# A gated cross-attention layer with a quantised feed-forward: first loads reordered, first query tiles in chunks, last batch's layers behind its last projection

## The chip, the cores and the metric

One core of a Trainium2 chip runs the whole program. Its engines are TensorE (PE; its weight loads are listed as PEld), VectorE (DVE), ScalarE (ACT), GpSimd (POOL) and SyncE (SP, which issues nearly all of the DMAs). The metric is the device time of one execution in microseconds.

## What is computed

For each of 16 batches of 512 tokens with 512 features, and 120 context rows of 384 features:

```python
q = layernorm(x) @ Wq + bq ; k = ctx @ Wk + bk ; v = ctx @ Wv + bv      # 16 heads of 32
x1 = x + tanh(g_xattn) * (softmax(q k' / sqrt(32)) v @ Wo + bo)
h = layernorm(x1) ; s = max(amax(|h|), 1e-6) / 127 ; z = round(h / s)  # per token
out = x1 + tanh(g_ffn) * ((z @ Wq8') * s * w_scale + bias)
```

## The kernel before

Every engine runs one list of instructions that is written out by hand; engines wait for each other by semaphores. A batch has 4 query tiles (or chunks) of 128 rows. `on`, `probs`, `xt`, `x_in`, `cen` and the two `x1` tiles are in SBUF, and there are 8 PSUM banks: `scores` (4), `pv_ps`, `sum_ps`, `bank_a`, `bank_b`. Products of float32 are made of three passes of a high and a low part (`three`, L315); the high part is a copy by ACT (`high_x`, `high_wq`), the low part a subtraction by DVE (`low_x`, L1008) or POOL (`wq_lo`, L1461).

The **front** (batch 0 and the preparation of batch 1) goes so. SP issues the loads in the order Wq, four tiles of `x` of batch 0, context, Wk, the transposed `x` (`xt`), and more behind it; ACT issues six small ones first, among them the gates and the biases. TensorE runs 22 float32 products of 128x128 that nobody reads (`keep_running`, L320), then the column means of Wq (L630). DVE makes the layernorm statistics of the four tiles (`x_statistics`, L981), then subtracts the means from Wq in four chunks (`centre_wq`, L994); POOL makes the reciprocal deviations, which TensorE spreads over the partitions (`spread_rstd`, L430). Keys of a pair of batches follow (`project_k`, L337), and as soon as `xt` has landed, DVE scales its chunks (`scale_x0`, L990), ACT and DVE split them, and `project_q(0, 0)` uses a chunk as it comes. `scores_by_query` (L354) gives the row maxima to DVE (`maxima`, L1018, on one set of score banks, so the next tile's scores wait for them). The maxima of all four tiles are split (`high_max`, `low_max`), turned by TensorE (`turn_max`, L362) and copied (`copy_max`), and `step(0)` starts with `scores_by_key` (L369, L373).

`step(i)`, for batches 0 to 14, holds the attention of batch i, the output projection and the quantised layer of batches i-1 and i-2, and the queries of batch i+1. In it POOL makes `q_xs` in two small operations per half batch (`quant_units`, L1334 and L1336). In step 0 `fold_bias` (L437) multiplies the value bias by Wo, for DVE (`fold_rows`) and for the residual loads of SP.

The **end** (`last_step`, `turns_and_layers`) has batch 15's attention and projection, and the quantised layers of batches 14 (m) and 15 (LAST). For each tile t of LAST: `residual` (L1036), statistics, `centre_last` (ACT, L753), `quant_max_last` (DVE), `quant_factors_last` (DVE), `round_last` (ACT, L758), `integers_last` (ACT, L763), `turn_last` (PE, L410), `copy_zt_last` (ACT, L767), `last_layer` (PE, L416), `dequantise_own` (DVE, L1083), and at the end `add_out_last` (DVE, L1089; tiles 1 to 3) or `add_own` (POOL, L1358; batch 14, and tile 0), and the store. Batch 14's second half is turned by `turn_z` (L404), copied by `copy_zt` (L773) and multiplied by `quantised_layer` (L422).

## Time and profile before

| | us |
|---|---|
| time, median of 3 runs | 850.18 |
| lowest and highest of them | 847.35, 850.35 |
| time of the profiled execution | 847.59 |
| its span, first to last instruction | 845.8 |
| TensorE busy in the span | 824.4 (97%) |
| DVE, ACT, POOL busy | 536.3, 512.1, 517.5 |
| mean granted TensorE clock | 0.998 of full |

The profiled execution is one execution, 2.6 us below the median; 1.8 us of its time lie outside the span. TensorE's busy share counts overlapped, modelled durations, so that it says little of single waits; those are read in the timeline.

### The profile page before, as it was taken

To read this page: it belongs to the slowest core of one execution; us is meant where nothing else is said; L and a number is where in the kernel's file an instruction comes from. 1 tells how busy PE (TensorE), PEld (TensorE's weight loads), DVE (VectorE), ACT (ScalarE), POOL (GpSimd) and SP (SyncE) were. 2 spreads that over 40 slices of the span, in tenths; PEclk is the share of its full clock that TensorE was granted. 3 is DMA by queue.
4 is the path that set the end of the run, shared out by engine and by line. 5 is a ranking of instruction groups with operands and counts; after the bars stand their busy time and mean duration, and the time that the engine had idled before them with its cause. 6 is when DMAs were issued, how large, how long until landed. Compare 5 with 4: busy or idle time off the path is not lost.

```text
span 845.8 us, 16173 instructions
## 1 busy us (share of the span) xinstructions
PE 824.4 (97%) x6356; PEld 518.8 (61%) x6356; DVE 536.3 (63%) x754; ACT 512.1 (61%) x711; POOL 517.5 (61%) x560
## 2 busy tenths in 40 slices
PE   8999999999999999999999999999999999999995
PEld 6755566656656656666666666656666666655553
DVE  5764658566567666558566566766657655555567
ACT  4465566665665656566566665666566565666674
POOL 3526475574767647495674768557485674655687
PEclk9999999999999999999999999999999999999999
DMA  8522604223241421314232241422315131111112
GB/s 323 165 54 97 193 26 137 76 87 107 68 132 52 153 77 38 126 51 155 76 97 83 76 138 50 138 76 60 121 51 162 38 89 50 38 51 50 51 51 100
DMA packets 39179, 79.62 MB, mean 94 GB/s; under 512 B 6848, under 2 KB 7488, under 8 KB 37056
## 3 DMA queue, kind: packets, MB, share of 16 engines
q1 hardware_dynamic: 37808, 77.74, 28.6%
q8 instruction: 50, 0.82, 0.4%
q10 hardware_dynamic: 1296, 0.86, 0.3%
q14 instruction: 25, 0.20, 0.1%
HBM read 61.78 MB, written 16.81 MB: 93 GB/s over the span
## 4 chain that ended last, share of the span: by engine, by line
PE 70%; DVE 15%; POOL 4%; issue 4%; ACT 3%; DMA 2%; SPq 1%; DVEq 0%; POOLq 0%; ACTq 0%
PE bank_b L315 22%; PE bank_a L315 12%; PE scores L354 8%; PE pv_ps L383 7%; PE sum_ps L385 6%; PE scores L369 5%; DVE row_max L1018 5%; DVE xt_lo L1008 4%; PE bank_a L422 3%; DVE u_sb L1096 2%; PE bank_a L337 2%; POOL x L1340 2%; DMA xt<-in_x_t 1%; PE scores L373 1%; PE bank_b L337 1%
## 5 line engine op out<-in xcount | busy, mean ns | idle before, releaser
L1018 DVE TENSOR_REDUCE row_max<-scores 128x16 f32<-128x1920 f32 x64 | 138.1, 2158 | 122.7 <-PE scores L354 122.7
L1353 POOL TENSOR_TENSOR x<-x,u_sb 128x512 f32<-128x512 f32 x56 | 75.6, 1350 | 159.4 <-DVE u_sb L1096 157.2
L715 ACT ACTIVATE probs<-scores 120x2048 f32<-120x2048 f32 x64 | 120.4, 1881 | 65.2 <-PE scores L373 64.9
L1344 POOL TENSOR_TENSOR o_lo<-on,o_hi 128x512 fp32r<-128x512 f32 x63 | 86.7, 1378 | 68.9 <-ACT o_hi L731 68.4
L1008 DVE TENSOR_TENSOR xt_lo<-xt,xt_hi 128x512 fp32r<-128x512 f32 x64 | 66.5, 1059 | 65.5 <-ACT xt_hi L678 65.3
L1348 POOL TENSOR_TENSOR x<-x,gbias_r 128x512 f32<-128x512 f32 x64 | 82.0, 1280 | 36.6 <-ACT cen L737 35.6
L1297 POOL TENSOR_TENSOR xt<-xt,rstd_b 128x512 f32<-128x512 f32 x60 | 92.6, 1571 | 3.4 <-ACT rstd_b L952 2.1
L354 PEld LDWEIGHTS scores<-k_sb,q_sb 32*128 32x128 f32 x2048 | 62.9, 186 | 51.7 <-issue 51.2
L1340 POOL TENSOR_TENSOR x<-x,gbo_r 128x512 f32<-128x512 f32 x64 | 89.5, 1409 | 1.2 <-DMA x<-in_x 1.0
L731 ACT ACTIVATE o_hi<-on 128x512 fp32r<-128x512 f32 x64 | 40.4, 632 | 73.2 <-DVE on L1031 73.0
L369 PE MATMUL scores<-q_sb,k_sb 32*120 32x512 f32 x512 | 72.6, 636 | 5.2 <-DVE row_max L1018 3.0
L354 PE MATMUL scores<-k_sb,q_sb 32*128 32x120 f32 x2048 | 74.7, 282 | 0.1
L721 ACT ACTIVATE inv_sum<-sum_ps 128x512 f32<-128x512 f32 x64 | 38.2, 597 | 56.7 <-PE sum_ps L385 56.7
L383 PE MATMUL pv_ps<-probs,v_sb 120*32 120x512 f32 x512 | 68.2, 605 | 1.9 <-ACT probs L715 0.3
L1047 DVE TENSOR_REDUCE q_amax<-cen 128x1 f32<-128x513 f32 x60 | 38.8, 683 | 44.3 <-POOL cen L1311 42.9
L385 PE MATMUL sum_ps<-probs,ones_f 120*32 120x512 f32 x512 | 66.6, 592 | 0.0
L742 ACT ACTIVATE cen<-cen,magic,q_rec 128x512 f32<-128x512 f32 x60 | 45.5, 806 | 31.3 <-DVE q_rec L1056 31.3
L315 PE MATMUL bank_a<-xt_hi,wq_hi 128*128 128x512 f32 x128 | 54.1, 423 | 1.2 <-DVE xt_lo L1008 1.0
L315 PE MATMUL bank_b<-xt_hi,wq_hi 128*128 128x512 f32 x128 | 53.8, 420 | 0.3
L315 PE MATMUL bank_b<-wo_hi,o_hi 128*128 128x512 f32 x124 | 53.1, 429 | 0.0
L373 PE MATMUL scores<-max_t,pick 8*120 8x512 f32 x256 | 51.9, 790 | 0.0
L315 PE MATMUL bank_b<-xt_hi,wq_lo 128*128 128x512 f32 x128 | 50.6, 395 | 0.0
(185 smaller groups left out, 1801.5 us busy)
## 6 DMA issues: line engine op xcount, KB each, us to landing
xt<-in_x_t SPq DMA_DIRECT2D x16, 1024.0 KB, 5.5
x<-in_x SPq DMA_DIRECT2D x64, 256.0 KB, 2.9
out_x<-x SPq DMA_DIRECT2D x61, 256.0 KB, 2.1
x_in<-in_x SPq DMA_DIRECT2D x60, 256.0 KB, 4.1
rstd_b<-rstd_rows SPq DMA_DIRECT2D x14, 256.0 KB, 4.9
ctx_sb<-in_ctx_t SPq DMA_DIRECT2D x8, 360.0 KB, 5.2
probs<-in_wq SPq DMA_DIRECT2D x1, 1024.0 KB, 5.7
x<-in_wo SPq DMA_DIRECT2D x1, 1024.0 KB, 11.7
```

The source lines that it names most:

```text
L315: ins = pe.matmul(out_ap, stat[a], mov[b], start=first and p == 0, stop=last and p == PASSES - 1)
L354: ins = pe.matmul(scores[:, r, t * KEYS:(t + 1) * KEYS], q_sb[STRIPS[r], j, t * P:(t + 1) * P], k_sb[n // 2 % 2][STRIPS[r], j, keys_of(n)] ...
L369: pe.matmul(scores[0:KEYS, r], k_sb[i // 2 % 2][STRIPS[r], j, keys_of(i)], q_sb[STRIPS[r], j], start=True, stop=False)
L383: pe.matmul(pv_ps[STRIPS[r], :], v_sb[i % 3][0:KEYS, h], probs[0:KEYS, r], start=True, stop=True)
L385: ins = pe.matmul(sum_ps[STRIPS[r], :], ones_f[0:KEYS, :], probs[0:KEYS, r], start=True, stop=True)
L715: act.activation(probs[0:KEYS], scores[0:KEYS], ACT.Exp, scale=SCALE).then_inc(p_ready, 1)
L1008: dve.tensor_tensor(xt_lo[:, c], xt[:, c], xt_hi[:, c].bitcast(F32), ALU.subtract).then_inc(x_split, 1)
L1018: dve.tensor_reduce(row_max[:].rearrange("p (t r) j -> p r t j", r=ROWG)[:, :, :, j], scores[:, :, 0:QT * KEYS].rearrange("p r (t k) -> p ...
L1297: pool.tensor_tensor(by_tile, by_tile, rstd_b[:].rearrange("q (p t) -> q t p", t=QT), ALU.mult).then_inc(x_scaled, 1)
L1340: pool.tensor_tensor(x1_of(n)[:, t], x1_of(n)[:, t], gbo_r[:], ALU.add).then_inc(xb_ready, 1)
L1344: pool.tensor_tensor(o_lo[i % 2][:, j], on[:, j % 2], o_hi[i % 2][:, j].bitcast(F32), ALU.subtract).then_inc(o_split, 1)
L1348: pool.tensor_tensor(x1_of(m)[:, t], x1_of(m)[:, t], gbias_r[:], ALU.add).then_inc(x1b_ready, 1)
```

## The change

- **Loads.** SP issues Wq, then the context, the left half of Wk (columns 0 to 255), the four tiles of `x`, the right half of Wk, `xt`. The biases, `picks` and the gates are no longer issued by ACT ahead of everything, but by SP behind `xt`. ACT's tanh of the gates moves from the start to behind the second query bias, with a table load on each side.
- **TensorE, front.** 14 unread products instead of 22. Keys of tiles 0 and 1 come before `spread_rstd(0)`. Query tiles 0 and 1 take turns chunk by chunk. The last chunk of the values of batch 1 moves behind `turn_max(0)`, the last chunk of `fold_bias` behind `turn_max(1)`.
- **DVE and ACT, front.** `low_x(1, 0)` moves behind `low_max(0)`; `high_max(0)` and `copy_max(0)` move ahead of `high_x(1, 2)` and `high_x(1, 3)`.
- **q_xs.** The division by 127 moves into the row `gws_r`, and one of POOL's two operations per half batch goes.
- **End.** The projection of LAST's tiles 2 and 3 comes before batch 14's quantised layers, with `turn_z` of batch 14's second half between the two. That half has a tile of its own (`zt_own`, in the free `k_sb`). LAST's quantisation takes its lower bound in `quant_factors_last` (three small DVE operations instead of two), so that `cen_last` needs no 513th column, and POOL loses four of its six small operations per tile. The eight dequantisations stand behind all of LAST's factors on DVE, and POOL's `add_own` behind all of its `bias_x1`.

```diff
@@ -230,11 +231,17 @@
     load(wq_landed, wq_stage[:], rows(wq))
+    load_ctx(0)
+    load(wk_landed[0], wk_sb[:, :, 0:D // 2], rows(wk)[:, :, 0:D // 2])
     for t in range(QT):
         load(x0_landed[t], x0_stage[t], x_v[0, t])
-    load_ctx(0)
-    load(wk_landed, wk_sb[:], rows(wk))
+    load(wk_landed[1], wk_sb[:, :, D // 2:D], rows(wk)[:, :, D // 2:D])
     load_xt(0)
+    load(bk_landed, bk_c[:], bk)
+    load(bq_landed, bq_c[:], bq)
+    load(picks_landed, picks[:], consts_pick)
+    load(gates_landed, gates[:, 0:1], g_xattn.partition_broadcast(P))
+    load(gates_landed, gates[:, 1:2], g_ffn.partition_broadcast(P))
     for t in range(QT):
@@ -416,6 +423,13 @@
+    def quantised_layer_own(m, t, bank):
+        pe.wait_ge(zt_ready, nth(m, 2, t // 2))
+        for c in range(DT):
+            at = ((t % 2) * DT + c) * P
+            ins = pe.matmul(bank[:], zt_own[:, at:at + P], w8_b[:, c], start=c == 0, stop=c == DT - 1)
+        ins.then_inc(ffn_done, 1)
@@ -430,13 +444,14 @@
-    def fold_bias(bank):
+    def fold_bias(bank, chunks):
         pe.wait_ge(wo_gated, 1)
         pe.wait_ge(bv_landed, 16)
-        for c in range(DT):
+        for c in chunks:
             ins = pe.matmul(bank[:], bv_c[:, c:c + 1].broadcast_to([P, P]), wo_stage[:, c],
                             start=c == 0, stop=c == DT - 1)
-        ins.then_inc(bv_ready, 1)
+            if c == DT - 1:
+                ins.then_inc(bv_ready, 1)
@@ -551,10 +566,12 @@
         if i == 0:
-            fold_bias(bank_b)
+            fold_bias(bank_b, range(DT - 1))
         if is_batch(b):
...
             turn_max(b, pv_ps)
+        if i == 0:
+            fold_bias(bank_b, range(DT - 1, DT))
         if is_batch(m):
@@ -594,51 +611,53 @@
             add_heads(i, t, DT - 1, scores[:, t]).then_inc(proj_done, 1)
+        project_o(i, 2, scores[:, 2])
+        pe.wait_ge(log_done, nth(i, DT, 3))
+        turn_z(m, 1, sum_ps)
+        project_o(i, 3, scores[:, 3])
+    def turns_and_layers():
+        m = LAST - 1
         quantised_layer(m, 0, bank_a)
+        pe.wait_ge(o_norm, nth(LAST, DT, 3))
+        turn_last(0, pv_ps)
         pe.wait_ge(x1_ready, nth(m, QT, 3))
         quantised_layer(m, 1, bank_b)
-        project_o(i, 2, scores[:, 2])
-        project_o(i, 3, scores[:, 3])
-    def turns_and_layers():
-        m = LAST - 1
-        pe.wait_ge(log_done, nth(LAST, DT, 3))
-        turn_z(m, 1, sum_ps)
-        pe.wait_ge(o_norm, nth(LAST, DT, 3))
-        turn_last(0, pv_ps)
         pe.wait_ge(x1_ready, nth(LAST, QT, 1))
-        quantised_layer(m, 2, scores[:, 1])
+        quantised_layer_own(m, 2, scores[:, 1])
+        turn_last(1, scores[:, 0])
+        pe.wait_ge(x1_ready, nth(LAST, QT, 2))
+        quantised_layer_own(m, 3, scores[:, 2])
+        pe.wait_ge(x1_ready, nth(LAST, QT, 3))
+        last_layer(0, scores[:, 3])
+        last_layer(1, sum_ps)
+        turn_last(2, pv_ps)
+        turn_last(3, scores[:, 0])
         pe.wait_ge(u_ready, nth(m, QT, 0))
-        quantised_layer(m, 3, bank_a)
-        turn_last(1, scores[:, 0])
+        last_layer(2, bank_a)
         pe.wait_ge(u_ready, nth(m, QT, 1))
-        last_layer(0, bank_b)
-        pe.wait_ge(x1_ready, nth(LAST, QT, 2))
-        last_layer(1, scores[:, 2])
-        turn_last(2, sum_ps)
-        pe.wait_ge(u_ready, nth(m, QT, 3))
-        last_layer(2, bank_a)
-        turn_last(3, pv_ps)
-        pe.wait_ge(x1_ready, nth(LAST, QT, 3))
-        last_layer(3, scores[:, 3])
+        last_layer(3, bank_b)
...
     pe.wait_ge(consts_ready, 5)
-    keep_running(22, pv_ps)
+    keep_running(14, pv_ps)
     pe.wait_ge(wq_landed, 16)
...
     ins.then_inc(wq_mean, 1)
-    pe.wait_ge(ident_landed, 16)
-    spread_rstd(0)
-    pe.wait_ge(wk_landed, 16)
     for j in range(DT):
+        pe.wait_ge(wk_landed[j // 2], 16)
+        if j == 2:
+            pe.wait_ge(ident_landed, 16)
+            spread_rstd(0)
         project_k(0, j, scores[:, j])
-    project_q(0, 0, bank_a)
-    project_q(0, 1, bank_b, first)
+    for c in range(DT - 1):
+        project_q(0, 0, bank_a, [c])
+        project_q(0, 1, bank_b, [c])
+    project_q(0, 0, bank_a, [DT - 1])
+    project_q(0, 1, bank_b, [DT - 1])
     pe.wait_ge(k_ready, nth(0, DT, 3))
     scores_by_query(0, 0)
-    project_q(0, 1, bank_b, second)
     project_q(0, 2, bank_a, first)
@@ -653,9 +672,10 @@
     project_v(0, bank_a, range(1, CT))
-    project_v(1, bank_b)
+    project_v(1, bank_b, range(CT - 1))
     pe.wait_ge(wq_centred, DT)
     turn_max(0, pv_ps)
+    project_v(1, bank_b, range(CT - 1, CT))
     pe.wait_ge(pick_ready, 1)
@@ -750,17 +770,21 @@
+    def copy_zt_own(m, h, bank):
+        act.wait_ge(z_turned, nth(m, 2, h))
+        act.activation(zt_own, bank[:].bitcast(BF16), ACT.Copy).then_inc(zt_ready, 1)
@@ -906,31 +930,24 @@
         integers_last(0)
-        centre_last(2)
+        copy_zt_own(LAST - 1, 1, sum_ps)
         round_last(1)
         integers_last(1)
-        copy_zt(LAST - 1, 1, sum_ps)
+        centre_last(2)
+        copy_zt_last(0, pv_ps)
         centre_last(3)
-        copy_zt_last(0, pv_ps)
+        copy_zt_last(1, scores[:, 0])
         round_last(2)
         integers_last(2)
-        copy_zt_last(1, scores[:, 0])
         round_last(3)
         integers_last(3)
-        copy_zt_last(2, sum_ps)
-        copy_zt_last(3, pv_ps)
+        copy_zt_last(2, pv_ps)
+        copy_zt_last(3, scores[:, 0])
         for k, t in enumerate(ADDED_LAST):
...
     load(ident_landed, ident_f[:], consts_f32)
-    load(gates_landed, gates[:, 0:1], g_xattn.partition_broadcast(P))
-    load(gates_landed, gates[:, 1:2], g_ffn.partition_broadcast(P))
-    load(bk_landed, bk_c[:], bk)
-    load(bq_landed, bq_c[:], bq)
-    load(picks_landed, picks[:], consts_pick)
-    act.wait_ge(gates_landed, 32)
-    act.activation(gates[:], gates[:], ACT.Tanh).then_inc(gates_ready, 1)
     act.preload_act_table_set("natural_log_exp_and_others")
@@ -947,6 +964,9 @@
     bias_q(0, 1, bank_b)
+    act.wait_ge(gates_landed, 32)
+    act.activation(gates[:], gates[:], ACT.Tanh).then_inc(gates_ready, 1)
+    act.preload_act_table_set("natural_log_exp_and_others")
     bias_q(0, 2, bank_a)
@@ -955,10 +975,10 @@
     high_x(1, 1)
+    high_max(0)
     high_x(1, 2)
+    copy_max(0, pv_ps)
     high_x(1, 3)
-    high_max(0)
-    copy_max(0, pv_ps)
     copy_v(1, bank_b)
@@ -1062,16 +1082,18 @@
         dve.wait_ge(cen_ready, nth(LAST, QT, t))
-        dve.wait_ge(last_pool, nth(t, 4, 3))
         dve.tensor_reduce(q_amax[:, t:t + 1], cen_last[t], AX.X, ALU.max,
...
         one = slice(t, t + 1)
+        dve.wait_ge(last_pool, nth(t, 2, 1))
         dve.wait_ge(amax_done, nth(LAST, QT, t))
-        dve.tensor_scalar(q_unit[:, one], q_amax[:, one], 1.0 / Q_MAX, 1.0, ALU.mult, ALU.mult).then_inc(last_steps, 1)
+        dve.tensor_scalar(xs_last[:, one], q_amax[:, one], x1_rstd[:, one], Q_EPS, ALU.mult, ALU.max).then_inc(last_xs, 1)
+        dve.wait_ge(last_xs, t + 1)
+        dve.reciprocal(rec_last[:, one], xs_last[:, one]).then_inc(last_steps, 1)
         dve.wait_ge(last_steps, nth(t, 2, 0))
-        dve.reciprocal(q_rec[:, one], q_unit[:, one]).then_inc(last_steps, 1)
+        dve.tensor_scalar(q_rec[:, one], rec_last[:, one], x1_rstd[:, one], Q_MAX, ALU.mult, ALU.mult).then_inc(last_steps, 1)
@@ -1211,10 +1233,8 @@
         x1_statistics(LAST, 1)
-        dequantise_own(m, 0, bank_a)
         quant_max_last(0)
         quant_factors_last(0)
-        dequantise_own(m, 1, bank_b)
         quant_max_last(1)
@@ -1223,16 +1243,18 @@
         quant_factors_last(2)
-        dequantise_own(m, 2, scores[:, 1])
         quant_max_last(3)
         quant_factors_last(3)
-        dequantise_own(m, 3, bank_a)
-        dequantise_own(LAST, 0, bank_b)
-        dequantise_own(LAST, 1, scores[:, 2])
+        dequantise_own(m, 0, bank_a)
+        dequantise_own(m, 1, bank_b)
+        dequantise_own(m, 2, scores[:, 1])
+        dequantise_own(m, 3, scores[:, 2])
+        dequantise_own(LAST, 0, scores[:, 3])
+        dequantise_own(LAST, 1, sum_ps)
         add_out_last(1)
...
         add_out_last(2)
-        dequantise_own(LAST, 3, scores[:, 3])
+        dequantise_own(LAST, 3, bank_b)
         add_out_last(3)
@@ -1258,9 +1280,9 @@
     maxima(0, 2)
-    low_x(1, 0)
     maxima(0, 3)
     low_max(0)
+    low_x(1, 0)
     low_x(1, 1)
@@ -1314,26 +1336,13 @@
-        pool.wait_ge(last_pool, nth(t, 4, 0))
+        pool.wait_ge(last_pool, nth(t, 2, 0))
         pool.tensor_tensor(x1_rstd[:, one], x1_var[:, one], half_neg[:, one], ALU.pow).then_inc(last_pool, 1)
-        pool.wait_ge(last_pool, nth(t, 4, 1))
-        pool.tensor_tensor(x1_std[:, one], x1_var[:, one], x1_rstd[:, one], ALU.mult).then_inc(last_pool, 1)
-        pool.wait_ge(last_pool, nth(t, 4, 2))
-        pool.tensor_scalar(cen_last[t][:, D:D + 1], x1_std[:, one], Q_EPS, 1.0, ALU.mult, ALU.mult).then_inc(last_pool, 1)
-    def quant_unit_last(t):
-        one = slice(t, t + 1)
-        pool.wait_ge(amax_done, nth(LAST, QT, t))
-        pool.tensor_tensor(q_top[:, one], q_amax[:, one], x1_rstd[:, one], ALU.mult).then_inc(last_top, 1)
-        pool.wait_ge(last_top, t + 1)
-        pool.tensor_scalar(xs_last[:, one], q_top[:, one], 1.0 / Q_MAX, 1.0, ALU.mult, ALU.mult).then_inc(last_xs, 1)
...
         pool.wait_ge(amax_done, nth(m, QT, 2 * h + 1))
-        pool.tensor_tensor(q_top[:, two], q_amax[:, two], x1_rstd[:, two], ALU.mult).then_inc(xs_top, 1)
-        pool.wait_ge(xs_top, nth(m, 2, h))
-        pool.tensor_scalar(q_xs[:, two], q_top[:, two], 1.0 / Q_MAX, 1.0, ALU.mult, ALU.mult).then_inc(xs_ready, 1)
+        pool.tensor_tensor(q_xs[:, two], q_amax[:, two], x1_rstd[:, two], ALU.mult).then_inc(xs_ready, 1)
@@ -1438,20 +1447,14 @@
         deviation_last(1)
-        quant_unit_last(0)
-        add_own(m, 0)
         bias_x1(LAST, 0)
-        quant_unit_last(1)
+        bias_x1(LAST, 1)
         deviation_last(2)
-        add_own(m, 1)
         deviation_last(3)
-        quant_unit_last(2)
-        bias_x1(LAST, 1)
-        quant_unit_last(3)
         bias_x1(LAST, 2)
-        add_own(m, 2)
         bias_x1(LAST, 3)
-        add_own(m, 3)
+        for t in range(QT):
+            add_own(m, t)
         add_own(LAST, 0)
```

Three places, as the instructions stand on their engines. SP from its start, before (`probs` holds Wq for now, `x_in` and `on` tiles of `x`):

```order
L188 DMA probs<-in_wq 128x4x512
L188 DMA x_in<-in_x 128x512 x2
L188 DMA on<-in_x 128x512 x2
L188 DMA ctx_sb<-in_ctx_t 128x720
L188 DMA wk_sb<-in_wk 128x3x512
L188 DMA xt<-in_x_t 128x2048
```

and changed:

```order
L189 DMA probs<-in_wq 128x4x512
L189 DMA ctx_sb<-in_ctx_t 128x720
L189 DMA wk_sb<-in_wk 128x3x256
L189 DMA x_in<-in_x 128x512 x2
L189 DMA on<-in_x 128x512 x2
L189 DMA wk_sb<-in_wk 128x3x256
L189 DMA xt<-in_x_t 128x2048
L189 DMA bk_c<-in_bk 128x4
L189 DMA bq_c<-in_bq 128x4
L189 DMA picks<-in_consts_pick 128x4
L189 DMA gates<-in_g_xattn 128x1
```

The context and half of Wk moved ahead of the tiles of `x`; the small loads stand behind `xt`. ACT, from the fourth query bias of batch 0 to the copied maxima, before:

```order
L697 ACTIVATE q_sb<-bank_b,bq_c 128x512
L678 ACTIVATE xt_hi<-xt 128x512
L701 ACTIVATE v_sb<-bank_a 120x512
L678 ACTIVATE xt_hi<-xt 128x512 x3
L705 ACTIVATE max_sp<-row_max 128x16x4
L709 ACTIVATE max_t<-pv_ps 128x512
```

and changed:

```order
L717 ACTIVATE q_sb<-bank_b,bq_c 128x512
L698 ACTIVATE xt_hi<-xt 128x512
L721 ACTIVATE v_sb<-bank_a 120x512
L698 ACTIVATE xt_hi<-xt 128x512
L725 ACTIVATE max_sp<-row_max 128x16x4
L698 ACTIVATE xt_hi<-xt 128x512
L729 ACTIVATE max_t<-pv_ps 128x512
```

Two of the three splits of batch 1's chunks moved behind the split of the maxima. TensorE, the end of the program, behind the last of LAST's projections, before:

```order
L404 MATMUL sum_ps<-ident_b,z_b 128x128 x8
L410 MATMUL pv_ps<-ident_b,xt 128x128 x4
L422 MATMUL scores<-w_b,zt 128x512 x4
L422 MATMUL bank_a<-w_b,zt 128x512 x4
L410 MATMUL scores<-ident_b,xt 128x128 x4
L416 MATMUL bank_b<-w_b,xt 128x512 x4
L416 MATMUL scores<-w_b,xt 128x512 x4
L410 MATMUL sum_ps<-ident_b,xt 128x128 x4
L416 MATMUL bank_a<-w_b,xt 128x512 x4
```

and changed:

```order
L436 MATMUL bank_a<-w_b,zt 128x512 x4
L417 MATMUL pv_ps<-ident_b,xt 128x128 x4
L436 MATMUL bank_b<-w_b,zt 128x512 x4
L430 MATMUL scores<-w_b,k_sb 128x512 x4
L417 MATMUL scores<-ident_b,xt 128x128 x4
L430 MATMUL scores<-w_b,k_sb 128x512 x4
L423 MATMUL scores<-w_b,xt 128x512 x4
L423 MATMUL sum_ps<-w_b,xt 128x512 x4
L417 MATMUL pv_ps<-ident_b,xt 128x128 x4
```

Two layers of batch 14 (`zt`) moved from before LAST's last projections to behind them, and `turn_z` (`z_b`) the other way.

## Rows read from the trace of the kernel before

**Rows 1.** The page, its first part: busy time, share, instructions of each engine.

```profile
PE 824.4 (97%) x6356; PEld 518.8 (61%) x6356; DVE 536.3 (63%) x754; ACT 512.1 (61%) x711; POOL 517.5 (61%) x560
```

**Rows 2.** Timeline 0 to 18: start, us, engine, line, operation, count [idle before <-releaser].

```profile
1.67 7.24 PE L320 MATMUL pv_ps<-inv_sum 128*128 128x128 f32 x44 [1.67 <-DVE magic L1242]
...
7.90 0.69 DVE L981 BATCH_NORM_STATS2 ln_stats<-x_in 128x6 f32<-128x512 f32 x1 [6.30 <-DMA x_in<-in_x]
...
8.75 3.60 PE L630 MATMUL pv_ps<-probs,inv_sum 128*128 128x512 f32 x8
...
12.38 2.48 DVE L994 TENSOR_TENSOR probs<-probs,pv_ps 128x512 f32<-128x512 f32 x4 [1.02 <-PE pv_ps L630]
...
13.45 5.03 PE L337 MATMUL scores<-ctx_sb,wk_sb 128*128 128x240 f32 x24
```

**Rows 3.** DMA issues of 0 to 16: count, KB each, us from issue to landing.

```profile
probs<-in_wq SPq DMA_DIRECT2D x1, 1024.0 KB, 5.7
```

**Rows 4.** Windows of PE: stretch, us, busy (count), granted clock, DMA share, GB/s.

```profile
6.00:7.00 1.00, 1.00 (x11) 1.00 0.49 125
...
10.00:11.00 1.00, 1.00 (x4) 1.00 1.06 394
```

**Rows 5.** Timeline 15 to 29.

```profile
15.89 1.29 DVE L990 TENSOR_TENSOR xt<-xt,sum_ps 128x512 f32<-128x512 f32 x2 [1.03 <-DMA xt<-in_x_t]
...
17.53 1.76 POOL L1461 TENSOR_TENSOR wq_lo<-probs,wq_hi 128x512 fp32r<-128x512 f32 x1
...
18.66 1.18 DVE L1008 TENSOR_TENSOR xt_lo<-xt,xt_hi 128x512 fp32r<-128x512 f32 x1
...
28.71 1.17 PE L354 MATMUL scores<-k_sb,q_sb 32*128 32x120 f32 x32
```

**Rows 6.** Timeline 36 to 44.

```profile
36.37 1.17 PE L354 MATMUL scores<-k_sb,q_sb 32*128 32x120 f32 x32
...
38.24 2.15 DVE L1018 TENSOR_REDUCE row_max<-scores 128x16 f32<-128x1920 f32 x1
...
39.64 1.66 ACT L678 ACTIVATE xt_hi<-xt 128x512 fp32r<-128x512 f32 x3
...
43.26 1.08 PE L369 MATMUL scores<-q_sb,k_sb 32*120 32x512 f32 x5 [0.78 <-ACT max_t L709]
```

**Rows 7.** Timeline 80 to 98.

```profile
87.09 1.08 PE L369 MATMUL scores<-q_sb,k_sb 32*120 32x512 f32 x5 [1.10 <-ACT max_t L709]
```

**Rows 8.** Groups of POOL's line 1336: count, ns min/median/max, first and last start.

```profile
L1336 POOL TENSOR_SCALAR q_xs<-q_top x30: 191/193/195, 113.1 to 820.0; 128x2 f32<-128x2 f32 x30
```

**Rows 9.** Timeline 825 to 846.

```profile
825.38 0.82 ACT L758 ACTIVATE probs<-probs,magic,q_rec 128x512 f32<-128x512 f32 x1 [1.28 <-DVE q_rec L1074]
...
831.73 1.58 PE L422 MATMUL scores<-w_b,zt 128*128 128x512 bf16 x4 [2.89 <-ACT zt L773]
...
842.21 0.90 DVE L1089 TENSOR_TENSOR x<-x,rstd_b 128x512 f32<-128x512 f32 x1
```

**Rows 10.** Groups of 822 to 846: count, busy us, mean ns, idle before.

```profile
L1089 DVE TENSOR_TENSOR x<-x,wk_sb 128x512 f32<-128x512 f32 x2 | 2.5, 1272 | 0.2
...
L753 ACT ACTIVATE probs<-x,x_mv 128x512 f32<-128x512 f32 x3 | 2.2, 718 | 1.8 <-DVE x_mv L1042 1.7
...
L1066 DVE TENSOR_REDUCE q_amax<-probs 128x1 f32<-128x513 f32 x3 | 2.1, 684 | 0.9 <-POOL probs L1322 0.9
...
L763 ACT ACTIVATE xt<-probs 128x512 bf16<-128x512 f32 x3 | 1.9, 630 | 0.1
...
L1083 DVE SCALAR_TENSOR_TENSOR q_sb<-bank_a,q_xs,gws_r 128x512 f32<-128x512 f32 x2 | 1.5, 742 | 0.0
L767 ACT ACTIVATE xt<-pv_ps 128x512 bf16<-128x512 bf16 x2 | 1.2, 592 | 1.4 <-PE pv_ps L410 1.4
...
L773 ACT ACTIVATE zt<-sum_ps 128x1024 bf16<-128x1024 bf16 x1 | 1.0, 1006 | 0.0
```

**Rows 11.** Windows of PE, as rows 4.

```profile
833.00:834.00 1.00, 1.00 (x4) 0.50 0.47 176
```

More of the change, by code:

```diff
@@ L106, in gated_layer @@
         ident_landed, picks_landed = sem("ident_landed"), sem("picks_landed")
-        bk_landed, wk_landed = sem("bk_landed"), sem("wk_landed")
+        bk_landed, wk_landed = sem("bk_landed"), [sem(f"wk_landed{h}") for h in range(2)]
         bq_landed, wq_landed = sem("bq_landed"), sem("wq_landed")
@@ L177, in gated_layer @@
         LAST = B - 1
-        cen_last = [flat(probs)[:, t * (D + 1):(t + 1) * (D + 1)] for t in range(QT - 1)] + [flat(x_in)[:, 0:D + 1]]
+        cen_last = [probs[:, t] for t in range(QT)]
+        zt_own = flat(k_sb[1 - LAST // 2 % 2])[:, 0:D].bitcast(BF16)
         z_last = [xt[:, t // 2, (t % 2) * (D // 2):(t % 2 + 1) * (D // 2)].bitcast(BF16) for t in range(QT)]
@@ L752, in centre_last @@
                 act.wait_ge(x1_mean, nth(LAST, QT, t))
-                act.activation(cen_last[t][:, 0:D], x1_of(LAST)[:, t], ACT.Identity, scale=-1.0,
+                act.activation(cen_last[t], x1_of(LAST)[:, t], ACT.Identity, scale=-1.0,
                                bias=x1_mv[:, t, 0:1]).then_inc(cen_ready, 1)
@@ L757, in round_last @@
                 act.wait_ge(last_steps, nth(t, 2, 1))
[L758 removed]
+                act.activation(cen_last[t], cen_last[t], ACT.Identity, scale=q_rec[:, t:t + 1],
                                bias=magic[:]).then_inc(scaled, 1)
```

19 lines of the change are left out of this document (9 added, 10 removed).

## The prediction

> **What bounds the kernel now.** The page's first part comes first: TensorE is busy for 97% of the span [rows 1], so that an edit in the middle of the program gives time only where TensorE stands still. The timeline then shows where it does: at the start, where most of what it does is unread products or waits for nothing that can be hurried by the middle, and at the end, where it stands 2.89 us before a layer of batch 14 and the last addition on DVE closes the program at 842.21 + 0.90 = 843.11 [rows 9]. The store behind that is the same in both kernels. Everything between step 0's start at 43.26 [rows 6] and the last batch is TensorE's own chain, so what the front gains arrives at the end whole. I sum front and end against the profiled execution, 847.59; the shown median, 850.18, is 2.6 us above it, and the difference that I find is taken off the median.
>
> **The middle.** `quant_units` loses one operation of 193 ns, 30 times [rows 8], 5.8 us of POOL in all. POOL is busy 61% [rows 1], and in these steps it next waits for DVE, so the sum takes 0; in each batch 0.39 us of POOL's order moves, which bounds it at 14 x 0.39 = 5.5 us either way if TensorE followed all of it (the slower side is rival D). Between steps 0 and 1 TensorE waits 1.10 us behind `turn_max(1)` for the copied maxima [rows 7]; the last chunk of `fold_bias` (one chunk of a float32 product is 3.60 / 4 = 0.90, rows of the column means [rows 2]) now fits into that. It gains the 0.90 only if the turn stood behind the product and not behind batch 0's last normalised tile; the turn needs that tile too, so I take 0. `fold_rows` on DVE now waits some 1.3 us (that chunk and the turn's 0.4) for the product, and three `low_x` are queued behind it; beside POOL they take up to 1.18 each [rows 5], moved behind its additions less, and TensorE has other chunks first: 0, bounds 0 to 0.5 lost.
>
> **The front, loads.** Wq needs 5.7 us from its issue to its landing [rows 3]. The tiles of `x` stand behind it, now also behind the context (360 KB) and half of Wk (384 KB). At the 394 GB/s of a full stretch [rows 4] that is 0.76 MB / 394 = 1.9 us. But the first tile lands about 1.5 us after Wq, and in the slice 6 to 7 only 125 GB/s move [rows 4]: 0.7 us of transfer are lost there. If that hole comes from the small loads that go with it, the delay is 1.25; I take the middle, 1.6. The Trainium skill (DMA: Bandwidth & Descriptors, Issuing engines are not separate DMA queues) says that DMAs issued by several engines run interleaved on the same 16 DMA engines, so that a second issuer saves only issue time; by it, moving the small loads to SP saves no transfer and the delay is 1.9.
>
> **The front, DVE.** Statistics start at 7.90, and the four chunks of `centre_wq` end at 12.38 + 2.48 = 14.86, with 1.02 of waiting for TensorE's means between [rows 2]. That wait goes: 14 unread products end at 1.67 + 14/22 x 7.24 = 6.3, Wq has landed about then, and the means, 3.60, are there at about 10.1. So centring ends at 7.90 + 1.6 + (6.96 - 1.02) = 15.4, 0.6 later. `scale_x0` starts at 15.89, after 1.03 us of waiting for `xt` [rows 5]; `xt` itself doesn't move much, since the bytes ahead of it are the same ones in another order (at most 0.7 earlier). So the scaling starts where it did, up to a delay of 1.95; beyond that it loses. Then `wq_lo` on POOL, one of them 17.53 + 1.76 = 19.29, runs 0.5 to 1 later beside `low_x(0, .)`, of which one (18.66 + 1.18 = 19.84) outlasts it by 0.55 [rows 5]. Two-input operations of DVE lose about 0.3 to 0.6 there when they meet one of POOL's: bounds 0.4 gained to 0.9 lost on the fourth chunk, and I take 0.3 lost. The key biases on ACT may wait up to 0.45 for their load, which now lands behind `xt`; nothing but the first scores wants them.
>
> **The front, TensorE.** Keys of tiles 0 and 1 end at about 10.1 + 2.5 = 12.6 (half of 5.03 [rows 2]). `spread_rstd`, now third, waits for statistics that are 1.6 late: it stood just ahead of the keys, which began at 13.45 [rows 2], so it is at about 14.6, and TensorE stands for 2.0 us. The other keys, 2.5 us, are done by 17.7, before the first chunk is split. Before, a wait of 2.89 us in the end was followed by a granted clock of 0.50 [rows 9, 11], 1.2 GHz; should that follow here too, the keys would take 5.0 and end at 20.2, beside chunks that come at DVE's pace: 0.3 lost at most.
>
> With tiles 0 and 1 chunk by chunk, six passes of tile 1 that stood behind `scores_by_query(0, 0)` are done before it, in gaps where TensorE waited for a chunk. But the next scores, at 28.71 [rows 5], then wait for the first `maxima`, an operation of 2.15 [rows 6] behind the first scores: they can start 0.65 earlier and not 1.4. Less the 0.3 of the chunk, that is **0.35** (-0.25 to 1.05). From there on DVE's `maxima` and TensorE's scores alternate as before. At the end of the front, tile 3's scores are done at 36.37 + 1.17 = 37.54, and their `maxima` start at 38.24 [rows 6], because `low_x(1, 0)` stands between: it goes, which gives 0.64 after the 0.06 that a signal takes. Two of the three splits (1.66 for three, from 39.64 [rows 6]) go out from ahead of `high_max`, which another 0.2 to 0.4 hangs on once the maxima are early; and the last chunk of the values of batch 1 fills the 0.78 before step 0 [rows 6]. TensorE can't win more than it stood still there, in the 0.78 and in a wait before the turn, so I take **0.9** (0.6 to 1.1). The two added table loads and the tanh on ACT stand before a query bias that waits for TensorE: 0. Front: 0.35 + 0.9 = **1.25** (0 to 2.0).
>
> **The end, ACT.** `round_last(0)` starts at 825.38 after 1.28 us of waiting for DVE's factor [rows 9]. Ahead of that factor went a dequantisation of 0.74 [rows 10] and a wait for POOL's column; one small operation (0.19, as POOL's in [rows 8]) comes in: it starts at about 824.7. From there ACT is one chain: round 0.82, integers 0.63, `copy_zt_own` 1.01, round 0.82, integers 0.63, centre 0.72, copy 0.59, centre 0.72 [rows 9, 10] = 5.94, with 0.2 between them: 830.85. DVE's maximum (about 0.7, as the 0.69 of the statistics over the same 512 columns [rows 2]) and three small operations end its factors at 832.15.
>
> **The end, DVE.** Now it is the bound. Six dequantisations of 0.742 [rows 10], with their gaps 4.5: 836.7. By then all four products of batch 14 and the first two of LAST are done, and the last two need ACT to 830.85 + 0.59 + 2 x 1.45 + 2 x 0.59 = 835.5 and TensorE one layer more, 1.58 even at the half clock [rows 9]: 837.1, in time for an eighth dequantisation at 838.6 or later. Two dequantisations and three additions are left: 1.5 + 3 x 0.90 = 4.2 if POOL lets them through, or 1.5 + 2 x 1.27 + 0.90 = 4.9 at the durations of before [rows 9, 10]. That is 840.9 or 841.65; POOL's `add_own`, five in a row from 832.9 (5 x 1.27 = 6.4, to 839.3), covers the first addition for certain and perhaps the second. I take 841.2, **1.9** before 843.11; the bounds are 1.0 and 2.2.
>
> The shared-port rule bears on this: an addition of 1.27 against one of 0.90 with the same shapes [rows 10] shows a collision of 0.37. The Trainium skill (SBUF — State Buffer, Who interferes with whom) says that a DVE instruction with two SBUF inputs contends with a GpSimd one that reads SBUF, and that the one issued first keeps the port for its whole length, which the trace fits. By the rule an addition can also lose nearly the whole of POOL's operation, once for each of the first two, and the end would gain 1.0 and not 1.9.
>
> **The sum.** 1.25 + 1.9 = 3.15, taken as 3.1: 847.59 - 3.1 = 844.5 for an execution like the profiled one, and 850.18 - 3.1 = **847.1** for the median.
>
> **Rivals.** A, the forecast: 847.1, between 845.8 and 848.3, chance 0.50. B, everything works: the hole in the transfers goes with the small loads, so that the centring is 0.35 earlier than I take and `xt` 0.7 earlier; the front gives 2.0 and the end 2.2: -4.2, **846.0**, 0.22. For it speaks the hole itself [rows 4]; against it, that a large load needs its own time to get under way wherever the small ones are. C, the front gives nothing: the tiles of `x` come over 1.95 us late, or the splits of `wq_lo` fall on `low_x` chunk after chunk, so that the first scores lose the 0.65 and more, and only the end pays: -1.9, **848.3**, 0.20. That the interleaved chunks don't do what they are meant for is in it: tile 1's low part has to come at TensorE's pace, and it comes at DVE's. D, slower: without POOL's second small operation its long operations start 0.2 us earlier in each half batch and get the port before DVE's two-input ones, as 1.27 against 0.90 shows that they can [rows 9, 10]. If one DVE operation that TensorE waits for loses 0.55 [rows 5] in each of the 14 batches, that is +7.7 - 3.1 = +4.6: **854.8**; it ends slower than before from 3.1 / 14 = 0.22 us a batch. Against it: TensorE stands still hardly anywhere in these batches [rows 1], so that a DVE operation mostly has slack. 0.08.
>
> **How the numbers follow.** The likeliest is A, 847.1. B's end with the bounds of both sums is -4.2 and somewhat more, C's with the end's lower bound is -1.0 and a front of -0.6 at worst; the runs of before are 3.0 us apart without the trace saying why, which I let widen the range a little at each side: 844.5 to 850.4, with D and half of the tails out. About 0.5%, 4.25 us, is what a measurement of this kernel tells from no change. Most of B lies just inside it at -4.2 and the scatter carries half across it, with a little of A: faster 0.25. Of D's 0.08, 0.05 is above +4.25: slower 0.05. The rest, 0.70, is within.
>
> **What would show it.** In the changed profile: the first statistic 1.2 to 1.9 later than 7.90, and no wait before `centre_wq`; the second tile's scores 0 to 1 before 28.71 with `maxima` as the releaser; step 0's first product at 42.0; the same distance from there to LAST's first residual as before; a round at about 824.7 less 1.25; DVE without a gap from the last factors to the last addition, which ends 3.1 earlier than at 843.11, at about 840.0. I am wrong if step 0 starts at 43.3 or later (C), if the distance between step 0 and the last batch changes by over 1 us (D), or if DVE waits for TensorE between the last dequantisations.

## The result, and the profile after

| | before | changed |
|---|---|---|
| median, us (runs) | 850.26 (4) | 843.06 (4) |
| lowest and highest | 847.35, 850.55 | 842.81, 844.04 |
| profiled execution | 847.59 | 844.04 |
| its span | 845.8 | 842.2 |

The ratio is 0.9931, interval 0.9914 to 0.9947: faster, by 7.2 us between the medians where 3.1 were forecast, and outside the range. The two profiled executions are only 3.55 apart. Both facts have to be explained: the profiled execution of before is 2.6 below its median, that of the changed kernel is the highest of its four. Measured from the profiled execution of before, the median of the changed kernel is 847.59 - 843.06 = 4.5 lower where 3.1 were forecast; the other 2.7 of the 7.2 are the distance between that profiled execution and its own median.

The changed kernel's timeline, start and end of the front (start, us, engine, line, operation, idle before and who ended it); it answers to [rows 2, 5, 6]:

```profile
9.09 0.69 DVE L1001 BATCH_NORM_STATS2 ln_stats<-x_in 128x6 f32<-128x512 f32 x1 [7.49 <-DMA x_in<-in_x]
...
12.30 2.45 DVE L1014 TENSOR_TENSOR probs<-probs,pv_ps 128x512 f32<-128x512 f32 x4
...
13.84 5.03 POOL L1464 TENSOR_TENSOR wq_lo<-probs,wq_hi 128x512 fp32r<-128x512 f32 x4
...
14.83 1.28 DVE L1010 TENSOR_TENSOR xt<-xt,sum_ps 128x512 f32<-128x512 f32 x2
...
16.31 3.10 DVE L1028 TENSOR_TENSOR xt_lo<-xt,xt_hi 128x512 fp32r<-128x512 f32 x1 [0.20 <-ACT xt_hi L698]
...
19.46 0.50 PE L322 MATMUL bank_a<-xt_hi,wq_hi 128*128 128x512 f32 x1 [2.40 <-DVE xt_lo L1028]
...
25.50 1.17 PE L361 MATMUL scores<-k_sb,q_sb 32*128 32x120 f32 x32 [0.19 <-issue]
...
42.78 1.08 PE L376 MATMUL scores<-q_sb,k_sb 32*120 32x512 f32 x5
```

The first statistic is 1.19 later and nothing is waited for before `centre_wq` (12.30). `xt` is there at least 1.06 earlier (its scaling starts at 14.83 against 15.89, and no longer waits for it), which was not forecast. And one subtraction, `low_x(0, 0)`, takes 3.10 us beside POOL's `wq_lo`, so that the first scores begin 1.32 later than at 24.18 in the trace of before, and step 0 only 0.48 earlier than at 43.26. The same subtraction in the repeated run of the changed kernel, whose trace is used below as well:

```profile
16.26 1.83 DVE L1028 TENSOR_TENSOR xt_lo<-xt,xt_hi 128x512 fp32r<-128x512 f32 x1 [0.20 <-ACT xt_hi L698]
```

The end, as [rows 9]:

```profile
823.91 0.82 ACT L778 ACTIVATE probs<-probs,magic,q_rec 128x512 f32<-128x512 f32 x1 [0.70 <-DVE q_rec L1096]
...
828.66 0.71 ACT L773 ACTIVATE probs<-x,x_mv 128x512 f32<-128x512 f32 x1
...
830.91 0.21 DVE L1096 TENSOR_SCALAR q_rec<-rec_last,x_rstd 128x1 f32<-128x1 f32 x1
831.04 0.74 DVE L1105 SCALAR_TENSOR_TENSOR q_sb<-bank_a,q_xs,gws_r 128x512 f32<-128x512 f32 x1
...
835.18 1.03 DVE L1111 TENSOR_TENSOR x<-x,wk_sb 128x512 f32<-128x512 f32 x1
...
838.64 0.91 DVE L1111 TENSOR_TENSOR x<-x,rstd_b 128x512 f32<-128x512 f32 x1
```

DVE works from its last factor to the last addition with no gap over 0.2, and ends at 839.55 instead of 843.11: the whole 3.55.

### The profile page after: what moved, and what is told of

It is laid out like the page before. It is cut to its first block, busy times and chain, and to the rows that moved or that the text cites. A ratio compares the mean times of both kernels' runs of the same rounds, so it can differ in the third digit from the quotient of the medians.

```text
span 842.2 us, 16102 instructions
## 1 busy us (share of the span) xinstructions
PE 822.0 (98%) x6340; PEld 517.5 (61%) x6340; DVE 533.7 (63%) x758; ACT 512.9 (61%) x712; POOL 507.2 (60%) x514
## 4 chain that ended last, share of the span: by engine, by line
PE 67%; DVE 16%; POOL 6%; issue 6%; ACT 3%; DMA 2%; SPq 0%; DVEq 0%; POOLq 0%; ACTq 0%
PE bank_b L322 21%; PE bank_a L322 11%; PE scores L361 7%; PE pv_ps L390 6%; PE sum_ps L392 6%; PE scores L376 5%; DVE row_max L1038 5%; DVE xt_lo L1028 3%; PE bank_a L436 3%; POOL x L1349 2%; DVE u_sb L1118 2%; PE bank_a L344 2%; DMA x_in<-in_x 2%; POOL x L1362 2%; POOL o_lo L1353 2%
```

## Where the other 3.6 us are: a second trace of before

The kernel before was run again beside the changed kernel, and beside each half of the change. The halves' edits, cut to a line or two (each has all the lines of its half):

```diff
# end_only
-                dequantise_own(m, 0, bank_a)
                 quant_max_last(0)
+                dve.tensor_scalar(xs_last[:, one], q_amax[:, one], x1_rstd[:, one], Q_EPS, ALU.mult, ALU.max).then_inc(last_xs, 1)
# front_only
-            keep_running(22, pv_ps)
+            keep_running(14, pv_ps)
```

> The kernel before, unchanged, for a second trace and more times. Its four times so far are 847.35 and three of 850.2 to 850.6, the changed kernel's 842.8 to 844.0, while the two profiled executions are only 3.55 apart (847.59 and 844.04). Theory S (the kernel before has two ways to run, 2.8 us apart, and mostly takes the slow one): times fall into two groups near 847.4 and 850.3, none between, and a trace of the upper group shows where the 2.8 lie. Theory R (scatter of the chip): times spread evenly over 847 to 850.5 and the changed kernel's do so too.

> The changed kernel, unchanged, on the same chip as the other three. Theory S: 842.8 to 844.1, one group, 6.5 to 7.5 below the kernel before's upper group. Theory R: a spread of 3 us.

> The kernel before with the end's part alone (order, own tile, factors on DVE, one operation of q_xs less); loads, unread products, chunks, tanh and the moves around the turned maxima are as before. From the two profiled executions the end is worth 2.98 us. If the slow way of running comes from the start of the program: two groups again, near 844.4 and 847.3. If it comes from POOL's operations in the middle, of which one goes here: one group near 844.4.

> The kernel before with the front's part alone. From the profiled executions it is worth 0.5 to step 0 and 0.2 more behind step 0: 846.8. If the slow way comes from the start of the program, only this remains of the groups: one group near 846.8. If it comes from the middle or the end, two groups near 846.8 and 849.6.

Measured on one chip: before 849.69 (20 runs, 847.46 to 852.5) and 850.06 (its copy, 12 runs), changed 843.01 (842.86 to 843.52), end alone 846.32 (844.84 to 847.34), front alone 846.01 (845.78 to 846.94). Theory S holds in that the spread of 3 us and more belongs to the kernel before and not to the chip; there are values between the groups, against its text. The end alone keeps a spread of 2.5, the front alone has 1.2: the slower executions go away with the front's part of the change, and not with the operation of POOL that the end's part takes away. Against 849.69 the end gives 3.4, the front 3.7, both together 6.7, so that nothing large lies in their combination. The front's 3.7 holds the disappearance of the slower executions too.

The copy's profiled execution is of the upper kind (span 848.5). Its distances to the first trace are taken at the product that turns a batch's maxima (`turn_max`). Step 0 begins 0.19 earlier than in the first trace, the turned maxima of batch 1 come 2.72 later, and from there the two traces keep that distance to the end. TensorE and DVE in between, first the faster trace of before, then the slower one (the answers for the two kernels are apart):

```profile
68.64 4.90 POOL L1297 TENSOR_TENSOR xt<-xt,rstd_b 128x512 f32<-128x512 f32 x3 [1.30 <-DMA xt<-in_x_t]
69.11 0.69 DVE L981 BATCH_NORM_STATS2 ln_stats<-x_in 128x6 f32<-128x512 f32 x1 [5.08 <-DMA x_in<-in_x]
69.94 0.54 DVE L998 TENSOR_SCALAR gws_r<-gws_r,gates 128x512 f32<-128x512 f32 x1
70.40 1.75 DVE L999 TENSOR_SCALAR gbias_r<-gbias_r,gates 128x512 f32<-128x512 f32 x1
74.28 1.13 PE L369 MATMUL scores<-q_sb,k_sb 32*120 32x512 f32 x8 [0.85 <-DVE row_max L1018]
```

```profile
68.34 4.71 POOL L1297 TENSOR_TENSOR xt<-xt,rstd_b 128x512 f32<-128x512 f32 x3 [1.20 <-DMA xt<-in_x_t]
69.51 0.69 DVE L981 BATCH_NORM_STATS2 ln_stats<-x_in 128x6 f32<-128x512 f32 x1 [5.93 <-DMA x_in<-in_x]
70.33 1.34 DVE L998 TENSOR_SCALAR gws_r<-gws_r,gates 128x512 f32<-128x512 f32 x1
71.59 1.74 DVE L999 TENSOR_SCALAR gbias_r<-gbias_r,gates 128x512 f32<-128x512 f32 x1
75.46 1.13 PE L369 MATMUL scores<-q_sb,k_sb 32*120 32x512 f32 x8 [2.51 <-DVE row_max L1018]
```

A tile of batch 3 lands 0.47 after POOL's scaling has begun in the one, 1.17 in the other. The two row operations of `gate_rows` stand behind its statistics. In the first trace `gws_r` still gets through early in POOL's row (0.54); in the second it comes 1.99 after that row's start and stands (1.34), and so does the next one. The maxima behind them (`row_max`) are late, and TensorE waits 2.51 instead of 0.85. Then its clock (windows of the slower trace: us, busy, granted clock, DMA share, GB/s; the first trace has 1.00 throughout):

```profile
76.00:78.00 2.00, 1.76 (x15) 0.81 0.00 0
78.00:80.00 2.00, 2.00 (x6) 0.50 0.00 0
80.00:82.00 2.00, 2.00 (x10) 0.83 0.00 0
```

The granted clock is half, 1.2 GHz, around 78 to 80. Of the 2.91 us (2.72 and the 0.19), 1.37 are there when the maxima are used (75.46 against 74.28, and 0.19), the other 1.54 come with the half clock. Whether moving the rows removes it:

```diff
+                if i == 0:
+                    gate_rows()
                 if is_batch(f):
                     x_statistics(f, 2)
-                if i == 0:
-                    gate_rows()
```

> The kernel before, with the two operations of gate_rows in step 0 put ahead of the statistics of batch 3's third tile, where DVE stands 5 us for that tile's load, and not behind them. In the slower trace of the kernel before these two take 1.34 and 1.74 beside POOL's scaling, the next maxima come late, TensorE waits 2.51 and then runs with a granted clock of 0.56 for 4 us. Theory G (the 2.8 us of the slower executions are this place): one group of times, at 846.6 (847.5 less most of the 0.85 that TensorE waits there in the faster trace), nothing above 847.8. Rival (the tile's late load is enough by itself, or the delay arises elsewhere): times still reach 849 and more.

> The changed kernel with the same move. Theory G: 0.94 of waiting goes, 842.1. Rival: the wait is turned into another one at once, 843.0.

Measured: 846.66 (846.36 to 847.13) and 841.87 (841.50 to 842.04), where the kernel before on the same chip gave 849.47 (847.38 to 851.03). Theory G holds in both. Neither trace has TensorE waiting before these products any more; in the first:

```profile
64.16 1.35 DVE L998 TENSOR_SCALAR gws_r<-gws_r,gates 128x512 f32<-128x512 f32 x1
65.43 1.52 DVE L999 TENSOR_SCALAR gbias_r<-gbias_r,gates 128x512 f32<-128x512 f32 x1
...
70.16 0.70 DVE L981 BATCH_NORM_STATS2 ln_stats<-x_in 128x6 f32<-128x512 f32 x1 [3.21 <-DMA x_in<-in_x]
```

With this place out of both kernels the change is worth 846.66 - 841.87 = 4.8. The place itself costs 849.47 - 846.66 = 2.8 before and 843.01 - 841.87 = 1.1 after. 4.8 + 2.8 - 1.1 = 6.5 is the distance of the medians, 849.47 - 843.01, split in three; it is the same numbers again and no further check. What is shown is that this move alone takes the upper group away from the kernel before (5 times, none above 847.13). The changed kernel with this move is faster than both (ratio to before 0.991, interval 0.9896 to 0.9923).

## Which part of the front does what

```diff
# after_small_back: the changed kernel with these lines of before again, and not behind xt
+    load(gates_landed, gates[:, 0:1], g_xattn.partition_broadcast(P))
+    load(gates_landed, gates[:, 1:2], g_ffn.partition_broadcast(P))
+    load(bk_landed, bk_c[:], bk)
...
# loads_only: the kernel before with
+            load_ctx(0)
+            load(wk_landed[0], wk_sb[:, :, 0:D // 2], rows(wk)[:, :, 0:D // 2])
...
# chunks_only: the kernel before with both of the two below; interleave_only: the first
+            for c in range(DT - 1):
+                project_q(0, 0, bank_a, [c])
+                project_q(0, 1, bank_b, [c])
# turn_only: the second, with fold_bias, high_max, copy_max and the last chunk
# of the values placed as in the change
             maxima(0, 2)
-            low_x(1, 0)
             maxima(0, 3)
             low_max(0)
+            low_x(1, 0)
```

> The changed kernel with the six small loads and the tanh back where the kernel before has them, everything else changed. If the full rate of the transfers between 5 and 10 us (398 GB/s against 290) comes from the small loads' move, it falls again, the tiles of x land 0.7 later and the time is up to 0.7 above 843.0; if it comes from the order of the large loads, it stays at 843.0. If moving them is also what keeps the kernel out of the slower executions, times reach 845.8.

> The kernel before with the loads' part of the change alone: new order of loads, small loads behind, tanh later, 14 unread products, keys ahead of the spread deviations. The chunk by chunk order, the moves around the turned maxima and the whole end are as before. If the loads bring the front's gain, 846.5 with no slower group; if the chunks and the moves around the maxima do (0.3 and 0.9 by the forecast), 847.5, and the groups of the kernel before, 847.5 and 850.3, remain.

> The kernel before with the chunk by chunk order of the first two query tiles and the moves around the turned maxima and fold_bias alone; all loads, the unread products and the keys' place are as before, and so is the end. With the loads changed too, step 0 began 1.5 earlier; with the loads alone 0.1 later. If the chunks and moves carry the gain: step 0 begins 1.2 earlier than at 43.26 and the time is 846.3. If they need the earlier chunks that the loads bring: 0.3 to 0.6 earlier, 847.0. On the slower executions: if the loads take them away, 849 and more still appears here; if a later order of DVE at the start of step 0 does, nothing lies above 847.5.

> The kernel before with query tiles 0 and 1 chunk by chunk and nothing else changed. In the changed kernel's trace the second scores begin 0.72 earlier than at 28.71 (the forecast said 0.35). If that is the interleaving's own: second scores at 28.0, step 0 at 42.5, faster executions at 846.8. The slower executions: if the moves around the turned maxima make them rarer, they are here as often as in the kernel before (over half of the times 2 us and more above the lowest).

> The kernel before with the moves around the turned maxima (low_x(1, 0) behind low_max(0), high_max and copy_max ahead of two splits, one chunk of the values behind the turn) and the split fold_bias, and nothing else changed. In the changed kernel's trace they are worth 0.83 up to step 0 (forecast 0.9): step 0 at 42.4, faster executions at 846.6. If these moves make the slower executions rarer: under a fifth of the times lie 2 us and more above the lowest; if not, over half.

The last column compares one product in each kernel's trace: the one that turns batch 0's maxima, which starts at 41.85 in the first trace of before. The kernel before, run beside them, had medians of 849.47 to 849.89.

| kernel | median | lowest to highest | turned maxima ahead of step 0, against before |
|---|---|---|---|
| changed, again | 843.01 | 842.86 to 843.52 | -1.54 |
| small loads back | 844.54 | 844.29 to 844.69 | 0.00 |
| loads only | 847.85 | 847.42 to 849.45 | +0.09 |
| chunks and turn only | 846.25 | 845.54 to 849.18 | -1.47 |
| interleave only | 850.07 | 847.18 to 852.11 | -0.62 |
| turn only | 849.98 | 849.54 to 851.11 | -1.12 |

**The small loads** are worth 1.5 us, twice the most that was expected. The windows from 5 to 10 us and from 15 to 20 without their move, and the first one with it (changed kernel):

```profile
5.00:10.00 5.00, 5.00 (x23) 1.00 0.88 290
15.00:20.00 5.00, 4.53 (x17) 0.66 1.05 397
```

```profile
5.00:10.00 5.00, 5.00 (x21) 1.00 1.05 398
```

108 GB/s for 5 us are 0.54 MB, 1.4 us of transfer: the hole of [rows 4] comes with the five small loads that were moved, 7 KB together (the sixth, the identity, stayed where it was). The move changes two things at once, the place of the small loads and the engine that issues them (ACT first of all, or SP behind `xt`), and no run takes them apart. ACT's tanh moves too, but ACT starts its next work, the first split of Wq, only when DVE has centred it (4.11 us of waiting), so it delays nothing there. With them back, the statistics begin at 10.40, `xt` is scaled from 16.37, TensorE stands 2.72 us before `spread_rstd`, and its granted clock falls to 0.66 on average, a mixture of both levels.

**The loads alone** give nothing up to step 0 (+0.09), though `xt` is an us earlier there too (scaling from 14.89): `low_x(0, 0)` stands 1.84 us beside `wq_lo`. **The chunks and the moves around the maxima** carry the gain up to step 0: 0.62, and 1.12 of which 0.08 were there before the moves. But turn only, 1.1 earlier at step 0, has all of its 12 times in the upper group; its trace shows 2.41 us of waiting for the maxima in step 0 and a granted clock of 0.50 from 76 to 80, and it loses 3.94 against the first trace of before from the turned maxima of batch 0 to those of batch 1. In the interleaved kernel's trace TensorE waits 2.24 there and the clock stays at 1.00; it loses 1.21, not 2.9. That is one value between the groups. TensorE's first product behind the late maxima, turn only and interleave only:

```profile
74.47 2.08 PE L369 MATMUL scores<-q_sb,k_sb 32*120 32x512 f32 x8 [2.41 <-DVE row_max L1022]
```

```profile
74.89 1.13 PE L369 MATMUL scores<-q_sb,k_sb 32*120 32x512 f32 x8 [2.24 <-DVE row_max L1020]
```

So a gain before step 0 was given back in step 0 by whatever let the tile land late.

**Why the changed kernel escapes is not settled.** Its two traces have the tile 0.56 and 0.51 behind POOL's start, and none of the 26 times of its kernels with `gate_rows` in place (changed, changed again, front only, small loads back, one column) lies 1.3 above the lowest of its own. With parts of the change, times of the upper kind (849 and more) are one of 11 (loads), one of 6 (chunks and turn), 7 of 12 (interleave) and 12 of 12 (turn), where the kernel before has 62 of 91. So they are seen less often with the loads' part, and with the chunks and the turn together (6 times are few). The place of the small loads is not what decides it: with them back none of 5 lies over 844.69. The four traces with a wait over 2 us (the copy of before and three of these) have the tile 1.14 to 1.28 behind POOL's start. No part removes the late landing for certain, and no row says why the tile comes late; the slower traces show the same issues.

The middle and the stall in the front were tried directly:

```diff
# qxs_only, on the kernel before
-                pool.tensor_scalar(q_xs[:, two], q_top[:, two], 1.0 / Q_MAX, 1.0, ALU.mult, ALU.mult).then_inc(xs_ready, 1)
# rows_early_lo_wait, on after_rows_early
                 pool.wait_ge(wq_hi_done, c + 1)
+                if c == 1:
+                    pool.wait_ge(x_split, 1)
# one_column, on the changed kernel (t = 3 of batch 14)
-  dve.scalar_tensor_tensor(out=(u_last if m == LAST else u_own)[t], in0=bank[:], scalar=factors[:, t:t + 1], in1=gws_r[:],
+  n = 1 if m < LAST and t == 3 else D
+  dve.scalar_tensor_tensor(out=(u_last if m == LAST else u_own)[t][:, 0:n], in0=bank[:, 0:n], scalar=factors[:, t:t + 1], in1=gws_r[:, 0:n],
```

> The kernel before with one POOL operation fewer in each half batch (30 of 193 ns), the division in gws_r. Forecast: the middle is worth 0, so the same groups of times as the kernel before, 847.4 to 850.6, and the distance from step 0's first product to the last turned maxima within 0.1 of the kernel before. Rival D: 3 us or more longer.

Measured: 848.34 (847.62 to 850.22), ratio 0.999, interval 0.998 to 0.9999. In its trace the distance to before is +0.86 at the turned maxima of batch 0, +1.11 at those of batches 1 and 2, and +1.19 at batch 15's. Over the stretch that the expectation named, from step 0 on, that is 0.33 and not within 0.1; but 0.25 of it arise in step 0, before the first `q_xs` (113.1 us [rows 8]), and the 13 steps that have the operation differ by 0.08. The middle is worth 0, and rival D has fallen. The +0.86 lies in the front, which this edit doesn't touch: the same program part comes out up to 0.9 apart between executions, which is another source of times between the groups.

> The changed kernel with gate_rows ahead of the statistics (841.9 by itself), and POOL waits with its second wq_lo until DVE has done low_x(0, 0), which stood 1.83 to 3.10 us for an operation of 0.68 while POOL ran. If that stall sets the first query product (18.1 to 19.5), it now begins at 17.1, the first scores 0.5 to 1.0 earlier, and the time is 841.2. Rival: wq_lo, 1.8 later, is then what the last chunks wait for: 841.9 or more.

Measured: 842.20 (842.11 to 842.43), 0.3 more than without the wait: the rival was right. DVE, timeline:

```profile
16.23 0.69 DVE L1028 TENSOR_TENSOR xt_lo<-xt,xt_hi 128x512 fp32r<-128x512 f32 x1 [0.20 <-ACT xt_hi L698]
...
17.44 1.48 DVE L1028 TENSOR_TENSOR xt_lo<-xt,xt_hi 128x512 fp32r<-128x512 f32 x1
...
19.44 2.89 DVE L1028 TENSOR_TENSOR xt_lo<-xt,xt_hi 128x512 fp32r<-128x512 f32 x2
```

The stall of the first subtraction has gone (0.69), and the three others now stand beside POOL (1.48, 2.89 for two). The collision is moved, not removed.

> The changed kernel; the dequantisation of batch 14's last tile is done on one column instead of 512, so that this tile's output is not computed. If DVE's row of dequantisations is what sets the end, the last addition comes 0.5 earlier: 842.5. If ACT or TensorE sets it, 843.0.

Measured: 842.93, against 843.01: nothing, though DVE had 0.53 less to do. Its first addition and POOL's row of additions, then the same addition in the repeated run of the changed kernel:

```profile
830.86 5.40 POOL L1368 TENSOR_TENSOR x<-x,q_sb 128x512 f32<-128x512 f32 x4 [0.24 <-DVE q_sb L1106]
...
833.58 1.55 DVE L1112 TENSOR_TENSOR x<-x,wk_sb 128x512 f32<-128x512 f32 x1
```

```profile
834.16 1.03 DVE L1111 TENSOR_TENSOR x<-x,wk_sb 128x512 f32<-128x512 f32 x1
```

It starts 0.58 earlier and takes 0.52 longer: both end at 835.1 to 835.2. So the time came out as for ACT or TensorE as the bound, but the addition did start earlier, which is against that. Shown is that the length of DVE's row of dequantisations doesn't set the end. What does is read from the rows: POOL's four additions take 5.40 / 4 = 1.35 each, so that the third ends at about 834.91 in the one trace and 834.96 in the other (its row starts at 830.91 there), and DVE's addition ends 0.2 behind that in both. That POOL's additions are the bound is therefore argued; no run changes them. The Trainium skill (SBUF — State Buffer, Who interferes with whom) states a contention of this kind, between a DVE instruction with two SBUF inputs and a GpSimd one that reads SBUF; here it shows as a fixed end and a variable length.

## Why the prediction was wrong, step by step

- **The offset between the profiled execution and the median.** "The difference that I find is taken off the median" is the step that failed. The 2.6 us were not an offset of every execution but a place in the kernel: 0.85 of waiting in the profiled execution, 2.51 with a half clock in the copy's, and 62 of 91 times of the kernel before lie over 849.0. None of the 26 times of the changed kernel and its near relatives is of that kind, so the two differences add. The prediction saw the spread ("3.0 us apart without the trace saying why") and only widened its range by it. Of the miss of 4.0 us (847.1 against 843.06) this step is 2.6 and the sum the rest, 4.5 in place of 3.1: 0.3 in the front, 1.1 in the end. On its own basis the forecast was -3.15 for executions like the profiled one, and the profiled ones came out at -3.55, which is luck in part: the changed kernel's was its slowest.
- **The middle, 0.** Right: 0.08 in 13 steps without POOL's operation. Between the turned maxima of batches 0 and 1 the changed kernel gains 0.17 to 0.27, which might be the chunk of `fold_bias`; but with `gate_rows` moved in both kernels it takes 42.20 there against 42.07, so 0, as taken, fits.
- **The loads.** Delay of the tiles 1.6 taken, 1.19 and 1.14 measured. The middle of the two bounds was the wrong place: the run with the small loads back shows that the hole goes with their move. The 1.9 that was worked out by the Trainium skill's rule (DMA: Bandwidth & Descriptors, Issuing engines are not separate DMA queues) is further off. That doesn't refute the rule, which is on who issues and not on the order; no run here separates the two. `xt` "doesn't move much, at most 0.7": it came at least 1.06 earlier.
- **The front, DVE.** 0.3 lost to collisions was taken. `low_x(0, 0)` takes 1.83 or 1.84 in the repeated run and five more traces with this order of loads, and 3.10 in the profiled one, against an undisturbed 0.69, so the us that `xt` won was lost at once. It is the term with the widest miss, and the two errors cancelled: in the repeated run first scores are 0.30 later, as forecast. In the profiled one they are 1.0 later than that, about what its time lies above the other three.
- **The chunks.** 0.35 forecast; second scores 27.99 in the repeated run, 0.72 earlier, 0.62 in the trace of the interleaving alone. The 0.65 was right and the 0.3 should not have been taken off: before, DVE began the first `maxima` at 25.86, 0.5 behind the end of the first scores, so that scores 0.3 later still find it in time (25.81). **The turn**, 0.9: 0.83 and 1.0. Front 1.25 forecast, 1.55 in the repeated run.
- **The end.** 1.9 forecast, and 2.2 the most; from batch 15's turned maxima (-0.58) to the last addition (-3.56) it is 2.98. The order of events was right, the lengths were not. ACT's chain from the first round to the last centring takes 829.37 - 823.91 = 5.46 and not 6.14: successive operations on ACT start before the row before them ends, and I added 0.2 of gaps. DVE's factors end at 831.12, 0.45 earlier than the forecast 832.15 less the 0.58 of that shift; from there the six dequantisations take, to the first addition, 4.14 and not 4.5 (0.66 apart, at 0.74 each), and the additions' stretch 4.37 and not 4.5. These are 0.94 of the 1.1.
- **The clock.** A wait of 2.0 before `spread_rstd` was forecast; 0.22 came, since the unread products ran until 7.9, not 6.3, and statistics were earlier. "14/22 x 7.24" took the products as equally long; their rows are not: up to 5.67 us both traces hold the same number of them in each microsecond (4, 7, 7, 6), then those of before come faster (9, 12, 12). The granted clock is 1.00 throughout, and no run says what makes the first ones slower.
- **The rivals.** B was nearest, with the hole in the transfers gone as it said and -4.2 in size: 847.5, the lower group of before, to 843.0 is -4.5. The parts agree less: the front gave 1.55 and not its 2.0, the end 2.98 and not its 2.2. C and D didn't occur.
